# Two of 18 probability blocks turned by TensorE and 16 by the DMA, in each step of a fused attention stage

## The reference

```python
scores = jnp.einsum('bqhd,bkhd->bhqk', xq, xk) * scale
causal = jnp.tril(jnp.ones((Tx, Tx), dtype=bool))
scores = jnp.where(causal[None, None], scores, -jnp.inf)
probs = jax.nn.softmax(scores, axis=-1)
out = jnp.einsum('bhqk,bkhd->bqhd', probs, xv).reshape(Bx, Tx, N_HEAD * HEAD_DIM)
return out @ wo
```

## Time and profile before

| | us |
|---|---|
| median of 3 runs (632.03 to 632.80) | 632.56 |
| the profiled execution | 630.89 |
| its span | 628.9 |
| busy PE, POOL | 563.0, 450.0 |
| busy DVE, ACT | 461.7, 434.7 |

### The profile page before, as it was taken

How to read it: one execution, slowest core, us unless ns; L and a number is a source line. 1 busy time by engine, 2 the same in 40 slices (tenths; PEclk the granted TensorE clock), 3 DMA queues, 4 the chain that set the end, 5 groups by cost and what they waited for, 6 DMA issues and landing times.

```text
span 628.9 us, 16324 instructions
## 1 busy us (share of the span) xinstructions
PE 563.0 (90%) x6880; PEld 484.8 (77%) x6880; DVE 461.7 (73%) x764; ACT 434.7 (69%) x601; POOL 450.0 (72%) x373
## 2 busy tenths in 40 slices
PE   5999999987889999999999999999999868774896
PEld 4878888966678888888888888888889757663475
DVE  4686757767768878878877887887888756519696
ACT  0624311268788898889879889888888897701894
POOL 3033436529989998998998999999999787724121
PEclk9999999999999999999999999999999999966799
DMA  9160004009999999999999999999999999950001
GB/s 288 49 200 0 2 22 88 2 22 164 192 171 196 183 197 193 188 194 215 191 190 190 199 205 193 193 187 190 192 199 193 184 191 207 186 108 0 1 26 43
DMA packets 317192, 91.75 MB, mean 146 GB/s; under 512 B 305984, under 2 KB 316224, under 8 KB 317120
## 3 DMA queue, kind: packets, MB, share of 16 engines
q1 hardware_dynamic: 311680, 86.66, 79.3%
q10 hardware_dynamic: 5440, 4.06, 2.4%
HBM read 13.11 MB, written 1.05 MB: 23 GB/s over the span
## 4 chain that ended last, share of the span: by engine, by line
PE 33%; POOL 23%; DVE 13%; DMA 13%; SPq 6%; ACT 6%; issue 5%; POOLq 0%; ACTq 0%; DVEq 0%
POOL p_lo L478 17%; PE PS L1154 11%; DMA pT_lo<-p_lo 10%; DVE small L1006 4%; PE PS L1413 4%; SPq L382 4%; PE PS L1287 3%; POOL roped L467 3%; SPq L386 3%; DMA pT_hi<-p_hi 2%; PE PS L1264 2%; PE PS L1269 2%; PE PS L1265 2%; ACT probs L656 2%; PE PS L1433 2%
## 5 line engine op out<-in xcount | busy, mean ns | idle before, releaser
L478 POOL TENSOR_TENSOR p_lo<-probs,p_hi 128x1280 f16<-128x1280 f32 (+7 forms) x128 | 303.6, 2391 | 35.2 <-DMA pT_lo<-p_lo 20.5
L656 ACT ACTIVATE probs<-PS,small 128x640 f32<-128x640 f32 (+7 forms) x256 | 173.6, 743 | 43.2 <-DVE small L1006 40.1
L1006 DVE TENSOR_REDUCE small<-PS 128x2 f32<-128x1280 f32 (+7 forms) x128 | 172.8, 1351 | 22.7 <-PE PS L1413 22.1
L665 ACT CAST p_hi<-probs 128x1280 f16<-128x1280 f32 (+7 forms) x128 | 145.4, 1159 | 4.8 <-DMA pT_hi<-p_hi 4.7
L1433 PE MATMUL PS<-v_hi,pT_hi 128*128 128x65 f16 x1152 | 78.9, 195 | 1.6 <-DMA pT_hi<-p_hi 1.6
L1437 PE MATMUL PS<-v_lo,pT_hi 128*128 128x64 f16 x1152 | 78.9, 195 | 0.0
L1433 PEld LDWEIGHTS PS<-v_hi,pT_hi 128*128 128x128 f16 x1152 | 74.1, 99 | 3.3 <-issue 1.1
L1413 PE MATMUL PS<-k_hi,q_hi 64*128 64x512 f32 (+3 forms) x384 | 74.0, 381 | 1.2 <-ACT probs L656 1.2
L1437 PEld LDWEIGHTS PS<-v_lo,pT_hi 128*128 128x128 f16 x1152 | 72.6, 98 | 0.4
L1413 PE MATMUL PS<-k_hi,q_lo 64*128 64x512 f32 (+3 forms) x384 | 66.1, 339 | 0.0
L1413 PE MATMUL PS<-k_lo,q_hi 64*128 64x512 f32 (+3 forms) x384 | 66.0, 339 | 0.0
(11 more groups left out here) (188 smaller groups left out, 1330.6 us busy)
## 6 DMA issues: line engine op xcount, KB each, us to landing
wgu_nat<-L_ffn_w_gate_up SPq DMA_DIRECT2D x2, 1024.0 KB, 9.6
wo_nat<-L_attn_wo ACTq DMA_DIRECT2D x8, 256.0 KB, 3.4
wkq_nat<-L_attn_wq ACTq DMA_DIRECT2D x6, 256.0 KB, 4.2
x<-L_attn_x SPq DMA_DIRECT2D x4, 256.0 KB, 3.8
wdn_nat<-L_ffn_w_down SPq DMA_DIRECT2D x1, 1024.0 KB, 11.3
wfc_nat<-L_ffn_w_fc SPq DMA_DIRECT2D x1, 1024.0 KB, 6.7
wpj_nat<-L_ffn_w_proj SPq DMA_DIRECT2D x1, 1024.0 KB, 9.7
pT_hi<-p_hi SPq DMA_TRANSPOSE x64, 5.6
```

The lines of the kernel that those rows point to most:

```text
L478: nc.gpsimd.tensor_tensor(p16_lo[G % 2][:, cols], probs[G % 2][:, cols], p16_hi[G % 2][:, cols], ALU.subtract).then_inc(p_lo_done, 1)
L656: nc.scalar.activation(probs[G % 2][:, start:start + w], PS[:, src:src + w], ACT.Exp, bias=nmax[:, 4 * (G % 2) + u:4 * (G % 2) + u + 1]).t ...
L665: nc.scalar.copy(p16_hi[G % 2][:, cols], probs[G % 2][:, cols]).then_inc(p_hi_done, 1)
L1006: nc.vector.tensor_reduce(nmax[:, first:first + 2], both_heads(G, part), AX.X, ALU.max, negate=True).then_inc(nmax_done, 1)
```

## The change

TURNED is 2. The first two blocks of a step's 18 (blocks 0 and 1 of part 0, head 0) are no longer cast, subtracted and transposed by ACT, POOL and the DMA. PE transposes them in 32 bits from probs into a bank of the ring (turn, a new job at the end of each step). ACT casts the transposed blocks from PSUM into pT_hi (turned_high, behind p_high(G, 0)). DVE subtracts that from PSUM into pT_lo (turned_low, in step G + 1 ahead of row_max(G + 1, 0)). p_high and p_low of part 0 start at column 256, and the DMAs take 16 blocks. pv waits for both new results, and the next users of the ring's bank wait for turned_low.

```diff
@@ sizes and ring
+        def part_range(G, part):
+            at = part_cols(G, part)
+            return slice(max(at.start, TURNED) * P, at.stop * P)
+        TURNED = 2
             RING += [(G, job(G, slot)) for slot in (1, 2) if job(G, slot)]
+            RING += [(G, "turn")]
@@ sync, likewise for the low half
-                sp.dma_start(pT_hi[G % 3][:], p16_hi[G % 2][:], transpose=True).then_inc(pT_hi_landed[G % 3], 16)
+                sp.dma_start(pT_hi[G % 3][:, TURNED:, :], p16_hi[G % 2][:, TURNED * P:],
+                             transpose=True).then_inc(pT_hi_landed[G % 3], 16)
@@ p_low on POOL, p_high on ACT
-                sl = part_cols(G, part)
-                cols = slice(sl.start * P, sl.stop * P)
+                cols = part_range(G, part)
@@ exp_unit on ACT
                     act.wait_ge(p_lo_done, 2 * (G - 2) + 2)
+                    act.wait_ge(turned, G - 1)
@@ ACT
+            def turned_high(G):
+                act.wait_ge(turned, G + 1)
+                nc.scalar.copy(pT_hi[G % 3][:, 0:TURNED, :],
+                               bank(side_bank(G, "turn"))[:, 0:TURNED * P].rearrange("p (b n) -> p b n", b=TURNED))\
+                  .then_inc(turned_hi, 1)
                 side(G, 2)
                 p_high(G, 0)
+                turned_high(G)
@@ DVE
+            def turned_low(G):
+                dve.wait_ge(turned_hi, G + 1)
+                nc.vector.tensor_tensor(pT_lo[G % 3][:, 0:TURNED, :],
+                                        bank(side_bank(G, "turn"))[:, 0:TURNED * P].rearrange("p (b n) -> p b n", b=TURNED),
+                                        pT_hi[G % 3][:, 0:TURNED, :], ALU.subtract).then_inc(turned_lo, 1)
                 side(G - 1, 2)
+                if G:
+                    turned_low(G - 1)
                 row_max(G, 0)
@@ PE
                     pe.wait_ge(landed[buf], 16 * turn)
+                    pe.wait_ge(turned_hi if pT is pT_hi else turned_lo, G + 1)
+            def turn(G, b):
+                pe.wait_ge(exp_done, 4 * G + 1)
+                for k in range(TURNED):
+                    last = nc.tensor.transpose(bank(b)[:, k * P:(k + 1) * P], probs[G % 2][:, k * P:(k + 1) * P], identf[:])
+                last.then_inc(turned, 1)
+                elif name == "turn":
+                    pe.wait_ge(turned_lo, G + 1)
                 side(G, job(G, 2))
+                side(G, "turn")
```

More of the change, by code:

```diff
@@ L233, in transformer_program @@
         p_hi_done, p_lo_done = sem("p_hi_done"), sem("p_lo_done")
+        turned, turned_hi, turned_lo = sem("turned"), sem("turned_hi"), sem("turned_lo")
         pT_hi_landed = [sem(f"pT_hi_landed{b}") for b in range(3)]
@@ L381, in transpose_hi @@
                 sp.wait_ge(p_hi_done, 2 * G + 2)
-                sp.dma_start(pT_hi[G % 3][:], p16_hi[G % 2][:], transpose=True).then_inc(pT_hi_landed[G % 3], 16)
+                sp.dma_start(pT_hi[G % 3][:, TURNED:, :], p16_hi[G % 2][:, TURNED * P:],
+                             transpose=True).then_inc(pT_hi_landed[G % 3], 16)
             def transpose_lo(G):
                 sp.wait_ge(p_lo_done, 2 * G + 2)
-                sp.dma_start(pT_lo[G % 3][:], p16_lo[G % 2][:], transpose=True).then_inc(pT_lo_landed[G % 3], 16)
+                sp.dma_start(pT_lo[G % 3][:, TURNED:, :], p16_lo[G % 2][:, TURNED * P:],
+                             transpose=True).then_inc(pT_lo_landed[G % 3], 16)
             for G in range(STEPS):
@@ L1056, in _ @@
             side(STEPS - 1, 2)
+            turned_low(STEPS - 1)
             for G in range(STEPS, STEPS + PV_LAG):
@@ L1489, in side @@
                     pv(G - PV_LAG, b)
+                elif name == "turn":
+                    turn(G, b)
                 elif name[:2] == "wo":
```

## The result

The changed kernel takes 671.55 us (671.40 to 671.57) against 632.29 before: ratio 1.0624, 95% interval 1.0606 to 1.0642. It is slower by 39 us; the forecast was 677, range 657 to 696. Its profiled execution took 671.4 us with a span of 669.3, 40.4 longer than before.

The account below looks back on a forecast made before the run. Several resources within 5% of each other (PE, POOL, ACT, DVE, DMA) were taken to hold the 6.45 us step. Middle +42.5, first group +4.1, first step +0.9, last group +4.0, end -6.8 gave 675.6, plus 1.7 to the median: 677 us (657 to 696).

Parts of the forecast that it names:

- The new wait: On DVE: turned_low waits for turned_high ahead of the next row maximum, 1 us or more in nearly all 64 steps.
- the loop: Row maximum, exponentials, cast, turned_high, turned_low, next row maximum, over DVE and ACT; 7.09 us a step without waits for PE.
- Relief at nothing: POOL's 0.49 us less a step and a ninth less DMA work, costed at nothing while something else sets the step.
- The first rival: Relief of POOL and DMA wins: steps stay at 6.45 us, only the end gains 6.8, 626 us; 4%.
- The sum: Changes by stretch: middle +42.5 us, first group +4.1, first step +0.9, last group +4.0, end -6.8; together +44.7.
- n = 1: Second step of eight in the middle: 7.40 us without waits for PE, 0.65 late for pv, 8.05 predicted.
- n = 5: Sixth step of eight in the middle: 6.77 us without waits for PE, 0.5 late, 7.27 predicted.
- PE's lateness: Late scores and pv on PE delay DVE's normalise, adding 1.95 us in eight steps, to 7.34 a step.
- n = 4: Fifth step of the last group, without rope jobs, counted at 6.2 us.
- the loop that it closes by itself: Rival: turn waits in the ring for DVE's reader behind the second maximum, delaying scores and pv; 716 us, half 695; 10%.
- bare count: Step lengths over DVE and ACT with no wait for PE: 56.75 us for eight steps, 7.09 a step.
- The last sign named for a wrong forecast: On PE: waits behind turn longer than the closed chain of row maximum, exponentials, cast, turned_high and turned_low.

Follow-up runs that it names:

- E2: Kernel before plus one wait: DVE waits for p_high(G - 1, 0) ahead of row_max(G, 0), no work added; 647.03 us.
- E8: Changed kernel with turned_high directly behind exponential 3, ahead of slot 2's cast and p_high(G, 0), and turned_low ahead of slot 2's work on DVE; 656.38 us.
- E5: Changed kernel in which ACT casts the turned blocks a second time, into a spare tile, ahead of turned_high in each step; 683.21 us.
- E3: Changed kernel's shorter casts, subtractions and DMAs without turn, turned_high, turned_low; pv multiplies block 2 in place of blocks 0 and 1; 620.54 us.
- E4: Changed kernel in which POOL also subtracts 256 columns into a spare tile once a step, ahead of p_low of part 0; 671.63 us.
- E11: Kernel before plus turn on PE, result unread and all 18 blocks still by DMA, issued behind the next step's scores of part 0; 641.42 us.
- E10: Kernel before plus turn on PE at each step's end, in the ring, result unread and all 18 blocks still by DMA; 660.08 us.
- E1: Changed kernel with turned_low(G - 1) one place later on DVE, behind row_max(G, 0) instead of ahead; 700.72 us.
- E9: Kernel before with PE transposing four blocks of a step in the last two of 64 steps alone; 628.13 us against 631.26.
- E6: Changed kernel with turned_low behind row_max(G, 0) and turn(G) behind the next step's scores of part 0; 670.14 us.
- E7: Changed kernel with turn(G) issued behind the next step's scores of part 0, orders on ACT and DVE kept; 674.07 us.

## Why the prediction was right, and where it was not

**The new wait lengthens the step: shown. That it decides alone: no.** DVE waits for pT_hi ahead of turned_low in all 64 steps, 75.9 us in all, 1.19 on average, where 1 us or more was forecast. The wait alone costs 16 us in the middle (E2); taking p_high out of the loop gives back 11 (E8), and 0.29 us more in it shows in four steps of eight (E5).

**Costs of the parts.** turned_high takes 0.386 and turned_low 0.425, taken at 0.40 and 0.43; two transposes take 0.22 in PE's queue (265.93 to 266.15 in the trace), as taken. From turned_high's start to the maximum's start the trace has 0.75 (268.17 to 268.92), predicted 0.77. POOL is busy 419.4 us, 30.6 less; 31 was predicted.

**Relief at nothing: right.** E3 gives 1.4 us in the middle, E4 0.02. The first rival falls, and with it the Trainium skill's preference for TensorE (VectorE: DVE Perf Modes, Rules for kernel authors) as a guide here: even with turn in its better place the transposes cost 11.5 us in the middle (E11), and what they relieve is worth 1.4. The Trainium skill's comparison (VectorE: DVE Perf Modes, The three transpose paths) is of each path's own time; here the ones relieved weren't what the step waited for.

**The sum.** Middle +39.0 (predicted +42.5), first group +3.8 (+4.1), last +4.6 (+4.0), end -6.7 (-6.8), and the start of the second step 0.2 earlier where 0.9 later was predicted: together +40.4 against +44.7. The first step itself is 0.9 longer, 6.96 against 6.08; but the first maximum starts 1.1 earlier, at 133.07 against 134.19, ahead of anything the change touches. In the experiments' traces it starts between 133.1 and 134.5. The terms that were off are n = 1, 0.24 too long, and n = 5, 0.36 too long: PE's lateness there was overestimated. In the last group n = 4 took 7.34 where 6.2 was counted; the others of this group were up to 0.2 shorter than counted. The clock is the likely cause. From 563 to 566 us the granted clock was 0.50 (the 1.2 GHz level), after PE had been busy for 0.31 and 0.08 of the two microseconds from 560 to 562. The scores of that step took long, and the normalise had to wait:

```profile
563.29 3.01 PE PS L1439 x13
...
568.21 0.18 DVE L1030 RECIPROCAL small<-PS 128x4 f32<-128x4 f32 x1 [1.21 <-PE PS L1460]
```

In E4 the clock fell at the same place, and the step took 7.37. In E5's same step (n = 4 of the last group) the clock was 1.00, the normalise waited for nothing, and the step took 6.31 in spite of the cast more. A low clock was in no sum of the prediction, which wanted it at 1.00 in the middle, where it was.

**The step that was wrong is how PE came into it.** The prediction put PE's wait in the ring behind the loop as a small addition, 1.95 us in eight steps or 0.24 a step, and gave the loop that it closes by itself 10% as a rival. E10 shows this second loop alone at 7.03 a step, next to 7.09 for the first by its bare count. The addition came out near what was measured (7.26 is 0.17 over 7.09) for another reason than the one given: a step pays for the later of the two and not for both. Taking in the second table the longer of the bare loop and E10 for each n gives 58.3 us for eight steps, measured 58.1, though single n differ by up to 0.4. So the closeness of the forecast is in part luck. The sums of the middle say the same: the middle grows by 15.9 with the wait alone (without the two new instructions), by 27.8 with PE's part alone, and by 39.0 with all, less than the 43.7 of the two. The last sign named for a wrong forecast, PE's waits behind turn longer than the loop, is all but met: a near tie of 7.03 and 7.09, and half of the steps each. The same mistake made E8's expectation 18 us too low, E10's 12, and E1's 56. E2, E3, E4, E9 and E11 lay in their ranges, E6 and E7 at the upper edge of theirs, and E5 3 us under its own, again because only half of the steps pay for the loop over ACT.

**Open.** Why PE's 11.5 us in E11 are what they are was not parted into queue time and other waits. E9's last group is 4 us longer than before. 2.9 of them fall in n = 5, ahead of the first of its two new steps, where its instructions are those of the kernel before: POOL waits 3.8 us for a landing of pT_lo there, PE stands idle from 529 to 531 us, and the granted clock is 0.50 from 533 to 535. Whether that varies from run to run was not tried.

## What to carry to other kernels

Where several engines are within a few per cent of each other, ask of an offload not what it relieves but which order it closes: a short instruction ahead of a long one on an in-order engine ties the long one to whatever the short one waits for. The wait with no work at all cost 0.33 us a step here (E2). Putting the short one behind is not safe either: here it made a longer loop over PE (E1). A new user of a ring of two buffers is a wait ahead of everything behind it in its queue; follow that wait round until it comes back to its start, and do this for each loop before adding the slower engine's cost. Work that clears a backlog pays only where the backlog is waited for: here four blocks in two last steps gave 3 us, two blocks in every step cost 39.

## What the runs showed that I had not expected

A place in a queue weighed more than the work put there: turn ahead of the scores or behind them is 660.1 against 641.4 us, with the same instructions; turned_low ahead of the maximum or behind it is 671.6 against 700.7. And DMA engines at a share of 1.16 in the middle, relieved of a ninth, gave 0.03 us a step (E3): a share over 1 was not a bound there.

The two loops take turns within eight steps. A single chain over one step, or one mean step, shows only one of them; the table by n and the chain over eight steps show both.
